# Opening of a fused Mamba-and-FFN layer: fewer idle products, transposes inside the f32 products, a later w_out load, weight sums on ScalarE, and step-size products of eight columns

## What is computed

```python
x = x + 0.5 * ffn(layernorm(x))          # 4-bit weights, dequantised, with a rank-16 LoRA and a bias
x = x + attn(layernorm(x))               # a Mamba-2 block, then a gated MLP (512 -> 1792 -> 512)
x = x + 0.5 * ffn(layernorm(x))          # the same ffn again

def ffn(n):
    W = (q - zeros[:, :, None]) * scales[:, :, None]        # groups of 64 inputs
    return n @ W.T + (1/16) * (n @ lora_A.T) @ lora_B.T + bias

def mamba2(h):                            # h = rmsnorm(x) * ln1_w
    z, xs, Bs, Cs, dt = split(h @ w_in.T) # 512, 128, 128, 512 and 4 columns
    xBC = silu(conv4(xs, Bs, Cs) + conv_b)
    dt = softplus(dt + dt_bias)           # the step size, 4 heads
    ...                                   # scan over chunks of 128 tokens with decay exp(-dt * exp(A_log))
    return (Y * silu(z)) @ w_out.T
```

## Time and profile before

| | |
|---|---|
| median of 3 runs | 766.98 us (766.56 to 767.13) |
| the profiled execution, its own time | 768.65 us |
| its span, first to last instruction | 766.9 us |
| PE busy | 755.4 us, 98% |
| DVE busy | 626.5 us, 82% |
| ACT busy | 446.4 us, 58% |
| POOL busy | 337.2 us, 44% |
| DMA | 71.86 MB, mean 94 GB/s |

### The profile page before, as it was taken

One profiled execution on the slowest core, in us unless ns is written; L12 is line 12 of the kernel. 1 busy time (PEld: TensorE's weight loads), 2 busy tenths in 40 slices (PEclk: granted clock), 3 DMA queues, 4 the chain that ended last, 5 costly groups with the idle time before them and its releaser, 6 DMA issues.

```text
span 766.9 us, 10654 instructions
## 1 busy us (share of the span) xinstructions
PE 755.4 (98%) x3469; PEld 353.2 (46%) x3470; DVE 626.5 (82%) x1230; ACT 446.4 (58%) x881; POOL 337.2 (44%) x392
## 2 busy tenths in 40 slices
PE   8999999999999999999999999999999999999998
PEld 3444554454555444444443444444444444444443
DVE  6888878878878979878799978878878878767994
ACT  3877767766686766643545556456456456444441
POOL 5631534663442379775413333233233233224574
PEclk9999999999999999999999999999999999999999
DMA  8843543552321211420521743743743743443565
GB/s 311 171 75 71 139 94 83 110 111 60 78 56 28 42 38 42 114 55 1 124 47 23 172 77 64 163 77 62 164 77 65 162 77 66 79 77 69 119 169 138
DMA packets 95414, 71.86 MB, mean 94 GB/s; under 512 B 65232, under 2 KB 72400, under 8 KB 95360
## 3 DMA queue, kind: packets, MB, share of 16 engines
q0 software_dynamic: 17280, 31.46, 23.0%
q1 hardware_dynamic: 77600, 39.66, 19.5%
q10 hardware_dynamic: 480, 0.07, 0.1%
HBM read 20.32 MB, written 4.19 MB: 32 GB/s over the span
## 4 chain that ended last, share of the span: by engine, by line
PE 77%; DVE 13%; ACT 4%; issue 3%; POOL 2%; DMA 1%; ACTq 0%; POOLq 0%; DVEq 0%
PE PS L1960 64%; PE PS L2083 4%; PE PS L2183 3%; DVE raw L1450 2%; PE PS L2091 1%; DVE stage L1450 1%; PE PS L2056 1%; DVE state L1432 1%; PE PS L2065 1%; DVE st L1289 1%; PE PS L2073 1%; PE PS L2048 1%; DVE xs L1382 1%; DVE S L1415 1%; DMA h<-lora_b_t 1%
## 5 line engine op out<-in xcount | busy, mean ns | idle before, releaser
L712 POOL DMA_DIRECT2D xs<-x x59 | 50.9, 864 | 151.2 <-ACT x L1159 137.1
L1960 PE MATMUL PS<-h,w_in 128*128 128x512 f16 x480 | 108.7, 379 | 0.2 <-issue 0.2
L1960 PE MATMUL PS<-h,x_t 128*128 128x512 f16 x408 | 94.0, 379 | 0.0
L1960 PEld LDWEIGHTS PS<-h,w_in 128*128 128x128 f16 x480 | 46.9, 98 | 65.3 <-issue 15.5
L1960 PE MATMUL PS<-n_T,stage 128*128 128x512 f16 x288 | 71.5, 379 | 0.0
L1159 ACT ACTIVATE x<-PS,d_d 128x512 f32<-128x512 f32 x59 | 40.2, 682 | 39.1 <-PE PS L1960 39.1
L1960 PEld LDWEIGHTS PS<-h,x_t 128*128 128x128 f16 x408 | 39.5, 98 | 48.5 <-issue 2.3
L521 POOL TENSOR_TENSOR r<-mv,mhalf 128x1 f32<-128x1 f32 (+1 forms) x32 | 29.4, 917 | 72.2 <-DVE mv L1293 55.0
L712 POOL DMA_DIRECT2D xs<-n x29 | 25.2, 868 | 71.1 <-ACT n L1159 60.8
L1960 PE MATMUL PS<-pre,stage 128*128 128x512 f16 x192 | 49.3, 379 | 0.0
L1129 ACT ACTIVATE xds<-tm,dgh 128x512 f32<-128x512 f32 x24 | 17.3, 722 | 53.0 <-DVE tm L1889 53.0
(11 more groups left out here) (314 smaller groups left out, 1819.3 us busy)
## 6 DMA issues: line engine op xcount, KB each, us to landing
xs<-x POOLq DMA_DIRECT2D x75, 256.0 KB, 3.3
xs<-n POOLq DMA_DIRECT2D x29, 256.0 KB, 3.3
x_t<-x_in SPq DMA_DIRECT2D x16, 256.0 KB, 3.0
x_t<-hb POOLq DMA_DIRECT2D x16, 256.0 KB, 3.8
out<-x_t SPq DMA_DIRECT2D x16, 256.0 KB, 2.3
raw_gu<-gate_t SPq DMA_DIRECT2D x7, 512.0 KB, 4.4
raw_gu<-up_t SPq DMA_DIRECT2D x7, 512.0 KB, 6.6
raw_d<-down_t SPq DMA_DIRECT2D x7, 512.0 KB, 7.3
```

What stands on the lines that cost most here:

```text
L712: po.dma_start(chunk_of(xs, c), d_tmps[d % 3], accum_op=ALU.add).then_inc(s_acc[d % 3], 16)
L1960: ins = pe.matmul(out_, lhs(a, b, k), rhs(a, b, k), start=first and n == 0, stop=last and n == len(todo) - 1)
```

## The change

1. The idle products before the first wait go from nine to eight, those ahead of `prologue()` from two to eight.
2. The selection products use 64 rows instead of 128 (`K_FFN`), so that fewer rows are cleared; `w_rows` is cleared by POOL instead of DVE, LoRA B is issued ahead of scales, both ahead of the first load of q; `lora_a` waits for two clears of POOL.
3. `first_f` is cut in two halves of two products, and the transpositions of the next chunks and the small maximum products stand between halves.
4. The bound of the ffn weight is the largest row sum of absolute values, taken by ACT (`ffn_sum`, four instructions), instead of the largest value, taken by DVE (`ffn_max`).
5. `build_dw` and `a_neg` on ACT go behind the first two pieces of `w_in_hi`; `w_in_hi` signals every block, `w_in_lo` waits for every block; `small_scales`, `x1_stats`, `lo1`, `max_row` change places on DVE; the scaling of `hb` goes ahead of `ln0(1)` on POOL.
6. `w_out` (1 MB) is loaded behind `next_x(1)` on SP's queue, instead of ahead of the four small loads.
7. `w_dt` holds the four dt columns of both parts side by side. `steps(i)` takes four products of eight columns with the high part and four of four columns with the low part for each chunk, 32 in all; `softplus(i, 0)` adds the two halves in two instructions instead of one.

The diff, cut to its core (`...` marks what is left out):

```diff
-N_WARM = 9
+N_WARM = 8
...
-N_SP = 16
+N_SP = 17
...
+        w_dt = sb("w_dt", [P, KB, 2 * H], F16)
...
-        R_LORA = 32
+        R_LORA, K_FFN = 32, 64
...
             load_x(0, 0)
-            load_q(0)
+            sp_.wait_ge(e_szero, 1)
+            sp_.dma_start(w_rows[R_LORA:R_LORA + RANK, :], lora_b_t).then_inc(s_la, 16)
             sp_.wait_ge(e_wzero, 1)
             sp_.dma_start(sc[0:NG, :], scales_t).then_inc(s_la, 16)
-            sp_.wait_ge(e_wzero, 2)
-            sp_.dma_start(w_rows[R_LORA:R_LORA + RANK, :], lora_b_t).then_inc(s_la, 16)
+            load_q(0)
             load_q(1)
...
-            sp_.dma_start(w_out[:, :, :], w_out_t.rearrange("(h p) n -> p h n", p=P)).then_inc(s_wout, 16)
...
             next_x(1)
+            sp_.dma_start(w_out[:, :, :], w_out_t.rearrange("(h p) n -> p h n", p=P)).then_inc(s_wout, 16)
             t1(0)
...
-            po.memset(sel_rows[32:64, :], 0.0).then_inc(e_szero, 1)
+            po.memset(w_rows[0:K_FFN, :], 0.0).then_inc(e_szero, 1)
+            po.wait_ge(e_szero, 1)
+            po.memset(sel_rows[R_LORA:K_FFN, :], 0.0).then_inc(e_szero, 1)
...
-            ln0(1, 1)
             po.wait_ge(s_hb, 16)
             chain(po.tensor_scalar(hb[:, :], hb[:, :], 0.5, None, ALU.mult))
+            ln0(1, 1)
...
+            def ffn_sum(k):
+                ac.wait_ge(e_wf, k + 1)
+                at = KB * NPROJ + k * DM
+                ac.activation(stage[:, :].bitcast(BF16)[:, at:at + DM], wf[:, k, :], ACT.Abs, accum_out=mxf[:, k:k + 1]).then_inc(e_wsum, 1)
...
-            ac.wait_ge(e_szero, 1)
+            ac.wait_ge(e_szero, 2)
             ac.dma_start(sel_rows[R_LORA:R_LORA + RANK, :], lora_a).then_inc(s_la, 16)
...
-            ve.memset(sc[:, :], 0.0).then_inc(e_wzero, 1)
-            ve.memset(w_rows[:, :], 0.0).then_inc(e_wzero, 1)
-            ve.memset(sel_rows[64:P, :], 0.0).then_inc(e_wzero, 1)
+            ve.memset(sc[0:K_FFN, :], 0.0).then_inc(e_wzero, 1)
...
-                for k in range(KB):
-                    chain(ve.tensor_reduce(mxf[:, k:k + 1], wf[:, k, :], AX_X, ALU.max, apply_absolute_value=True))
                 ve.tensor_reduce(mx[:, 0:1], mxf[:, :], AX_X, ALU.max).then_inc(e_max, 1)
...
             def w_in_lo(n):
-                ve.wait_ge(e_whi, n + 1)
                 piece = W_IN_PIECES[n]
                 for k in range(KB):
+                    ve.wait_ge(e_whi, n * KB + k + 1)
...
+                if n == 1:
+                    chain(last)
+                    ve.tensor_copy(w_dt[:, :, 0:H], w_in[0][:, :, NPROJ - H:NPROJ])
+                    last = ve.tensor_copy(w_dt[:, :, H:2 * H], w_in[1][:, :, NPROJ - H:NPROJ])
...
-                    last = product(PS[:, B_TB, DT_AT + j * H:DT_AT + (j + 1) * H],
-                                   lambda a, b, k: h2T[a][:, k, (i * CH + j) * P:(i * CH + j + 1) * P],
-                                   lambda a, b, k: w_in[b][:, k, NPROJ - H:NPROJ], KB)
+                    at, tokens = DT_AT + j * 2 * H, slice((i * CH + j) * P, (i * CH + j + 1) * P)
+                    for k in range(KB):
+                        pe.matmul(PS[:, B_TB, at:at + 2 * H], h2T[0][:, k, tokens], w_dt[:, k, :], start=k == 0, stop=False)
+                    for k in range(KB):
+                        last = pe.matmul(PS[:, B_TB, at:at + H], h2T[1][:, k, tokens], w_dt[:, k, 0:H], start=False, stop=k == KB - 1)
...
-            first_f(0)
+            first_f(0, 0)
             first_t0(2)
-            first_f(1)
+            first_f(0, 1)
+            first_f(1, 0)
             max_turn(0)
+            first_f(1, 1)
             first_t0(3)
-            first_f(2)
+            first_f(2, 0)
             max_spread(0)
-            first_f(3)
+            first_f(2, 1)
+            first_f(3, 0)
+            first_t0(4)
+            first_f(3, 1)
             max_turn(1)
-            first_t0(4)
+            first_f(4, 0)
+            first_t0(5)
             max_spread(1)
-            first_f(4)
-            first_t0(5)
-            first_f(5)
-            keep_warm(2)
+            first_f(4, 1)
+            first_f(5, 0)
+            first_f(5, 1)
+            keep_warm(8)
```

More of the change, by code:

```diff
@@ L917, in w_in_hi @@
                 for k in range(KB):
-                    last = ac.activation(w_in[0][:, k, piece], raw_in[:, k, piece], ACT.Copy, scale=lsw[:, k:k + 1])
-                last.then_inc(e_whi, 1)
+                    ac.activation(w_in[0][:, k, piece], raw_in[:, k, piece], ACT.Copy, scale=lsw[:, k:k + 1]).then_inc(e_whi, 1)
             def fold(g):
@@ L1028, in _ @@
             tc0(1)
+            ffn_sum(0)
+            ffn_sum(1)
+            hi0(2, 2)
+            ffn_sum(2)
+            ffn_sum(3)
+            tc0(2)
+            hi0(3, 3)
+            w_in_sum(0)
+            w_in_sum(1)
+            w_in_sum(2)
+            tc0(3)
+            w_in_sum(3)
+            hi1(0, 0)
+            hi0(4, 0)
+            tc0(4)
+            hi1(1, 1)
+            hi0(5, 1)
+            hi1(2, 2)
+            tc0(5)
+            hi1(3, 3)
+            ac.wait_ge(e_scale, 1)
+            w_in_hi(W_IN_PIECES[0])
+            w_in_hi(W_IN_PIECES[1])
             ac.wait_ge(s_head, 48)
@@ L1032, in _ @@
             build_dw(0)
-            hi0(2, 2)
             build_dw(1)
             build_dw(2)
-            tc0(2)
-            w_in_sum(0)
-            hi0(3, 3)
-            w_in_sum(1)
-            tc0(3)
-            hi1(0, 0)
-            w_in_sum(2)
-            w_in_sum(3)
-            hi1(1, 1)
-            hi0(4, 0)
-            tc0(4)
-            hi1(2, 2)
-            hi0(5, 1)
-            hi1(3, 3)
-            tc0(5)
-            ac.wait_ge(e_scale, 1)
-            w_in_hi(W_IN_PIECES[0])
-            w_in_hi(W_IN_PIECES[1])
             def dn_hi(p):
@@ L1311, in ffn_weight, with ffn_bound @@
                 ve.scalar_tensor_tensor(wf[:, k, :], bank(z), LORA_SCALE, wf[:, k, :], ALU.mult, ALU.add).then_inc(e_wf, 1)
[L1313 to L1316 removed]
+            def ffn_bound():
+                ve.wait_ge(e_wsum, KB)
                 ve.tensor_reduce(mx[:, 0:1], mxf[:, :], AX_X, ALU.max).then_inc(e_max, 1)
@@ L1572, in softplus @@
                     ve.wait_ge(e_dt_mm, i + 1)
-                    ve.scalar_tensor_tensor(four(v), four(PS[:, B_TB, DT_AT:DT_AT + NT]), d_i[:, :], rep(dtb), ALU.mult, ALU.add).then_inc(e_spx, 1)
+                    both = PS[:, B_TB, DT_AT:DT_AT + 2 * NT].rearrange("p (c a h) -> p c a h", c=CH, a=2)
+                    ve.scalar_tensor_tensor(four(v), both[:, :, 1, :], d_i[:, :], rep(dtb), ALU.mult, ALU.add).then_inc(e_spx, 1)
+                    ve.wait_ge(e_spx, base + 1)
+                    ve.scalar_tensor_tensor(four(v), both[:, :, 0, :], d_i[:, :], four(v), ALU.mult, ALU.add).then_inc(e_spx, 1)
                 elif k == 1:
-                    ve.wait_ge(e_spx, base + 1)
+                    ve.wait_ge(e_spx, base + 2)
                     ve.tensor_scalar(m, v, -1.0, None, ALU.mult).then_inc(e_spx, 1)
                 elif k == 2:
-                    ve.wait_ge(e_spx, base + 2)
+                    ve.wait_ge(e_spx, base + 3)
                     ve.tensor_tensor(m, m, v, ALU.min).then_inc(e_sp_neg, 1)
@@ L1749, in step @@
                     bound_row(1)
+            clear()
             prep0(0, 0)
             zero_rows()
-            clear()
             ffn_weight(0)
@@ L1760, in _ @@
             prep0(3, 3)
-            ffn_max()
+            ffn_bound()
             x1_stats(0, 0, B_P[0])
+            x1_stats(1, 1, B_P[1])
             max_row(0)
-            x1_stats(1, 1, B_P[1])
-            lo1(0, 0)
             prep0(4, 0)
@@ L1768, in _ @@
             w_in_bound()
+            lo1(0, 0)
+            prep0(5, 1)
+            x1_stats(3, 3, B_P[1])
+            max_row(1)
             lo1(1, 1)
-            prep0(5, 1)
-            max_row(1)
-            x1_stats(3, 3, B_P[1])
             both_scales()
@@ L1775, in _ @@
             lo1(3, 3)
+            x1_stats(4, 0, B_P[0])
             w_in_lo(0)
-            x1_stats(4, 0, B_P[0])
-            small_scales()
             w_in_lo(1)
             x1_stats(5, 1, B_P[1])
+            small_scales()
             prep0(6, 2)
@@ L2174, in first_t0, with first_f @@
                 last.then_inc(e_n0_tr, 1)
-            def first_f(c):
-                pe.wait_ge(e_n0T, c + 1)
-                if c - 1 > 0:
-                    pe.wait_ge(e_x1, c - 1)
-                for k in range(KB):
+            def first_f(c, half):
+                if half == 0:
+                    pe.wait_ge(e_n0T, c + 1)
+                    if c - 1 > 0:
+                        pe.wait_ge(e_x1, c - 1)
+                for k in range(2 * half, 2 * half + 2):
                     if c == 0:
@@ L2183, in first_f @@
                     last = pe.matmul(bank(B_P[c % 2]), nT32[c % 2][:, k, :], wf[:, k, :], start=k == 0, stop=k == KB - 1)
-                last.then_inc(e_ffn, 1)
+                if half == 1:
```

(1 more changed line is left out.)

31 lines of the change are left out of this document (15 added, 16 removed).

## The result

The kernel after takes 771.95 us (median of 19 runs, 767.64 to 776.90) against 767.15 for the kernel before on the same chip (19 runs, 766.46 to 767.76): ratio 1.0069, interval 1.0045 to 1.0092. Forecast were 764.6 and faster; it is slower by 0.7%, outside the range. The spread itself has changed.

| group | runs of 31 | time | recorded granted clock over the span |
|---|---|---|---|
| A | 6 | 767.57 to 767.90 | 1.000 |
| B | 12 | 769.17 to 772.73 | 0.993 to 0.998 |
| C | 13 | 775.15 to 777.44 | 0.999 or 1.000 |

What follows compares the result with a forecast made beforehand. PE's own work was taken as the bound, with the opening ending on PE or the last DMA transposition. Opening 1.1 plus steps 1.6 less 0.3 made 2.4 us, 766.98 to 764.6; range 763.5 to 766.3.

Steps and rivals of the forecast that it cites:

- Columns are unchanged; I price the eight selection products at the same 0.86.: Opening on PE: selection products on 64 rows cost 0.86 us each, the same as with 128.
- third rival: Clock stays low through the half-row selection products until 24.4: 5 us slower, 772; chance 6%.
- The earlier start: Start of PE's opening: LoRA loads issued earlier, first selection product at 4.8 instead of 6.30, 1.5 us earlier.
- the 2 us that weren't counted: Opening on PE: an earlier clock rise returns up to 2 us; nothing in the sum, up to 0.5 in the range.
- The wait for chunk 1: Opening: second chunk waits for `hb`, its transposition not before 12.5; nothing counted in the sum.
- Net gain 0.9: Opening on PE: transpositions inside the f32 products remove waits for ACT's copies; 0.9 us net, from 0.5 to 1.3.
- Chunk 3 goes at 37.5 to 37.7 and lands at 40.7.: Last DMA transposition of the opening: issued and landed at these times, so PE's own end at 41.5 decides.
- the late case: Chunk 2's issue takes 2.48 us again; chunk 3 lands at 41.9, `proj(0, 0)` starts at 42.2; 765.3, chance 25%.
- 1.1 us for the opening: End of the opening: `proj(0, 0)` starts at 41.5 instead of 42.60, 1.1 us earlier, bounds 0.4 and 1.8.
- I take the difference off the median.: Whole kernel: savings summed against the profiled execution of 768.65 are subtracted from the median of 766.98.
- The step products: Stages: 32 products in 0.81 us instead of 48 in 1.22; 1.6 us saved over four stages.
- a wait at chunk 7: Stage work after the opening: ACT and DVE close behind PE at its ffn product; 0.3 us taken off the gain.

Runs made afterwards that it cites:

- experiment 3: Kernel before with only the selection products cut to 64 rows: seven executions at 766.73 to 767.86 us, five at 776.73 to 777.04.
- experiment 2: Kernel after with all 128 rows back in the selection products, the added rows holding zeros: median 767.53 us, ratio 1.0012.
- experiment 5: Kernel after with 24 idle products at the start instead of 8, half rows kept: median 770.04 us, ratio 1.0034.
- experiment 8: Kernel after with full rows, w_out and the first chunk's high and low parts at their earlier places: median 768.18 us, ratio 1.0013.
- experiment 9: Kernel after with full rows, w_out, the first chunk's parts and GpSimd's order all as in the kernel before: median 767.05 us, ratio 0.9999.
- experiment 12: Kernel after with only GpSimd's order as in the kernel before, half rows kept: median 768.86 us, ratio 1.0038.
- experiment 4: Kernel before with the eight-column step products alone: median 766.19 us against 767.17, ratio 0.9990.
- experiment 10: Kernel before plus step products, `first_f` in halves and the order of calls of after: 767.54 us against 767.20, ratio 1.0005.
- experiment 7: Kernel after with full rows and the load of w_out at its earlier place: median 767.64 us, ratio 1.0006.
- experiment 11: Kernel before plus step products, split `first_f`, and `x1_stats(3)` ahead of `max_row(1)` on VectorE: 768.26 us against 767.24, ratio 1.0007.
- experiment 14: Kernel before with the eight-column step products alone, a second series: median 766.44 us against 767.24, ratio 0.9989.
- experiment 6: Kernel after with full rows and the first chunk's high and low parts at their earlier places: median 767.31 us, ratio 1.0007.

## Why the prediction was wrong

**"Columns are unchanged; I price the eight selection products at the same 0.86."** This is the step that failed. With 64 rows the price has two values, 0.86 and 1.71, by the clock. Experiment 3 shows the effect alone and experiment 2 its absence; in experiment 5 a clock brought up by other work stayed up in all five executions. The prediction had a clock that stays low as its third rival, with 772 at 6 in 100. Its mechanism is that of group C, its price too small: 5 us, where group C lies 8 to 10 above before. It let the level rise at 24.4 (it rose between 26 and 27 in that trace), and it took 2.0 us off for a slow start of before that most executions of before don't seem to have. That the measured median is 771.95 is luck: it is an execution of group B, in which a clock that is up falls again, and no part of the prediction had that. Its chance for the slow side was far too low: two rows of that very trace, products at 1.7 to 1.8 us behind nine idle ones, said that the clock was still open when the selection products began.

The Trainium skill (TensorE: Matmul & The Clock Gate, Part 1) states that the gate has two levels and that the moment of the rise differs from run to run. Both agree with the 0.50 and 1.00 of group B's rows and with the groups. The Trainium skill, in the same part, puts the penalty of the rise below 1% of a typical kernel span. Here it is 8.8 of 766 us between the traces of groups C and A, 1.1%.

**The earlier start** came as forecast in the trace of group A (4.77); in the nine traces with the new order of the loads it lies between 4.63 and 5.55, so 4.8 was on the early side. In six of them PE waits for LoRA A, issued at 1.91 in each and landed 2.9 to 3.6 us later; the quicker landing near 4.0 that the prediction also weighed occurs in none. In group A the clock even returned the 2 us that weren't counted. The wait for chunk 1 was seen (forecast 12.5, measured 12.69) and priced at nothing in the sum. Two pairs of kernels put GpSimd's new order, which makes this wait, at about 1 us (medians of experiments 8 and 9, best groups of after and experiment 12).

**"Net gain 0.9" for the transpositions inside the products** was right on PE's own path: from the first f32 product to the idle products PE takes 24.31 us in the trace of experiment 2 (14.63 to 38.94) and 25.22 in that of experiment 4 (14.54 to 39.76), and the wait for `hi0(5)`, forecast at 0.4, is 0.44. It does not reach the end, because the last DMA transposition decides there. On ACT's order of before the same move costs about 1 us (experiment 10), by a wait for `hi0(4)`.

**"Chunk 3 goes at 37.5 to 37.7 and lands at 40.7."** PE's own end was right, 41.5; the other was mis-sized by 0.7 us at the issue and by 1.0 on the way to the landing, 42.3 in all, where even the late case had 41.9. So 1.1 us for the opening became 0.05 later. w_out, priced at nothing, is not the cause (experiment 7). The traces show a path that the prediction left out. PE's timeline, then DVE's, of the kernel after:

```profile
33.46 0.66 PE L2188 MATMUL PS<-ident,n 128*128 128x128 f32 x4 [0.44 <-ACT n L769]
34.05 0.38 PE L2209 MATMUL PS<-mx,tri 1*128 1x1 f32 x2
```

```profile
34.46 0.16 DVE L1343 COPY mxa<-PS 128x2 f32<-128x2 f32 x1 [0.56 <-PE PS L2209]
36.24 0.70 DVE L1374 TENSOR_TENSOR h2n_p<-hn,h2n_p 128x512 f16<-128x512 f32 x1
```

The second `max_spread` now stands behind the transposes of chunk 5 and runs at 34.05, in experiment 4 at 31.09. DVE waits for it, makes both scales, and only then `lo1(2)` (36.24, in experiment 4 34.15). SP issues chunk 2 right behind that (36.96) and chunk 3 right behind chunk 2 (38.31), 0.8 us after `lo1(3)` had ended at 37.5. The nine traces with the split and the clock up throughout all show this order of events, with chunk 2 issued between 35.5 and 37.7 against 34.9 in experiment 4. No run moved `max_spread` alone, so this is read from traces and not shown by an experiment.

**"I take the difference off the median."** The trace of before was an execution of 768.65 whose clock rose at 10.4. Its projection began at 42.60; the same opening with the clock up, and with LoRA B landed 0.5 us earlier, began at 41.13 (experiment 4). 766.9 less 1.47 is a span of 765.4, 767.1 with the 1.7 around it: the median. So most executions of before seem to have had already what the forecast still hoped to win there; all four traces of this opening with full rows in experiments 4, 10, 11 and 14 have the clock up from the first selection product, but no trace of before itself does. Against them the opening of after is 1.5 us later in its best group, and the steps bring it back to 0.5 behind: 767.7 against 767.15.

**The step products** were right: 0.80 for 0.81, 1.64 in four stages. Behind them one wait grew, that of PE for ACT at the last maximum:

```profile
PE PS L2139 <- ACT raw L887: 0.8, 1, 0.8
```

It was 0.5 in the kernel before (0.52 at 253.71, now 0.82 at 252.45). The account from trace to trace closes there: 0.05 for the opening, less 1.64, and 0.30 for this wait make 1.29 us earlier, measured 1.26. At the end 1.0 is left; where the last 0.26 went was not traced. The prediction took 0.3 off for a wait at chunk 7. That wait is 0.22 in both kernels, so its size was right by luck; it does appear where PE came earlier (0.33 and 0.99 in experiments 4 and 14).

**Open.** What makes one execution of half rows start slow and another not: the moment of the first selection product doesn't sort them (fast at 4.77, 5.00 and 5.55, slow at 5.04 and 5.61). Group B: with half rows 16 of 43 executions of this opening show a recorded clock of at most 0.998 (after and experiment 12), with full rows 5 of 57 (experiments 2 and 6 to 9), one of 11 in experiment 11, none of 12 in experiment 3 and none of 5 in experiment 5. Half rows make the fall likelier, the wait in front of the second transposes isn't needed for it, and why the order of before was spared is not settled. To fill the wait with full-row idle products wasn't tried.

## What to carry to other kernels

A matmul cut to fewer rows saved no time here while its columns stayed, and near the start of a kernel it can leave the clock low for as long as such products last. Keep full rows, with zeros if need be, until the clock is up, and look at more than one execution: a spread that grows from 1 to 9 us is a result of its own.

Before an opening is costed, ask which of the possible executions the trace shows; a saving against a slow one may be there already in the median. And when work is moved between two halves of an operation, or a small product behind a larger one, what it waits for is then waited for by everybody behind it.

## What the hardware showed unexpectedly

- Rows count even when they hold zeros: the 64 rows that experiment 2 adds do, and the median falls from 772.41 to 767.53.
- Products that alternate between 64 and 128 rows are a little slower than with 128 throughout, at the full clock: 2.49 against 2.21 us for the same stretch (group A and experiment 2).
- The low level can last past 26 us with PE busy throughout: 13.0 of 13.0 us between 12 and 25 in the execution of experiment 3.
- A clock that is up can fall while half-row products run, to 0.50 for about 3 us. It costs 1.7 us: from the second transposes to the eight f32 products is 6.40 us in group B's trace (13.85 to 20.25) and 4.75 in group A's (12.69 to 17.44). The spans differ by 2.5, because group B's trace is already 1.2 us late at the transposes.
- The same DMA transposition, the last of the opening, took 3.0 us from issue to landing in the kernel before, 4.0 in the one after, 3.0 in experiment 10 and 4.2 in experiment 4, each time with another issued 1.3 to 2.5 us ahead of it; what sets the difference is not shown.
